# 32-wide pair attention: another order of scores and maxima on TensorE, and one buffer of probabilities in place of two

## The chip, the cores and the metric

The program runs on one core of a Trainium2 chip. The metric is the device time of one execution in microseconds, the median of the runs shown. Times are those of one hardware profile of the kernel before, unless said otherwise.

## What is computed

A decoder of two layers, each of attention, cross attention and a feed-forward part. The change touches the two self-attention cores, with 16 heads of width 32 over 4 batches of 512 positions, which per layer amount to:

```python
B, S, D, NH, HD = 4, 512, 512, 16, 32
# layer 0: one key and one value head shared by the 16 query heads; layer 1: 16 key and value heads
scores = jnp.einsum('bqhd,bkd->bhqk', Q, K) / sqrt(32)      # layer 1: 'bthd,bshd->bhts'
attn = jax.nn.softmax(scores, axis=-1)
out = jnp.einsum('bhqk,bkd->bqhd', attn, V)
```

## The kernel before

The program is a row of stages with a barrier between them; on each engine the order is written out by hand and held together by semaphores. The stage in question is `attend` (lines 376 to 666). It runs twice: tiles `l0s_...` in layer 0, `l1s_...` in layer 1. It works on 32 pairs of heads (`NP = 32`), each pair being one *step* `p`. For a pair, TensorE does

- 8 maximum matmuls (`maximum`, L460): queries by keys, 128 queries x 512 keys, two into each of the two halves of `max_bank`. VectorE reduces two of them at a time to row maxima (L604), four reductions a pair;
- `max_rows` (L470): 4 small matmuls that turn the negated maxima into two rows, which ScalarE copies into the query tile (L579), so that the score matmul subtracts them;
- 8 score matmuls (`score`, L481): keys by queries, transposed, 128 keys x 512 queries, k = 0 to 7. Even k (the pair's first head) goes to `score_bank0`, odd k to `score_bank1`. ScalarE takes the exponential of each (L590) into the probabilities `pT`;
- 4 weighings (`weigh`, L491, kt = 0 to 3), two fp32 matmuls each (every one has two rows in the profile), which multiply the values by `pT` of one block of 128 keys and add up in `o_bank`;
- `turn` (L503): 4 transposes of the result, which VectorE had copied out (`take_oT`, L622) and then divides by the sums and stores or adds (L630, L634, L640).

The work is pipelined over pairs. In step `p` TensorE works on the scores of `p`, the maxima of `p + 2`, the rows of `p + 1`, and the last weighings and the turn of `p - 1`. The steps run as 4 straight ones, a loop of 6 rounds with 4 steps (p = 4 to 27), and 4 straight ones. The last two steps have no maxima, since no pair is left. A step has two halves, which I call A (k = 0 to 3) and B (k = 4 to 7):

```python
for k in range(4):          # half A
    score(p, s, k)
    m(k)
max_rows(p + 1, ...); weigh(p - 1, ..., 2); weigh(p - 1, ..., 3)
for k in range(4, 8):       # half B
    score(p, s, k)
    m(k)
turn(p - 1); weigh(p, s, 0); weigh(p, s, 1)
```

Before each score TensorE waits until the exponential of two scores earlier has left the score bank: `pe.wait_ge(exp_done, 8 * p + k + 1)`, the counter having been started at 2. ScalarE waits for each score (`scored`), and at k = 0 also for `weighed`, the count of pairs whose last weighing is done, before it overwrites `pT[s % 2]`.

Of the kernel before, what the change touches and what calls it, by code (L numbers as in the profile page):

```python
# [374 lines left out]

def attend(st, name, q_dram, k_dram, v, per_head, out):

    nc = st.nc  # L380
    NP = B * NH // 2
    scale = HD ** -0.5
    STK = 3 * HD
    R = 4
    W = 2 * HD
    maxed, max_read, ms_ready, mrow_turned, mrow_ready, scored, exp_done, weighed, oT_ready, turned, o_read = st.sems(
        "maxed", "max_read", "ms_ready", "mrow_turned", "mrow_ready", "scored", "exp_done", "weighed", "oT_ready",
        "turned", "o_read")
    max_hi_done, rden_done, on_done, ks_made, vs_cleared, vs_made, v_staged, ms_cleared = st.sems(
        "max_hi_done", "rden_done", "on_done", "ks_made", "vs_cleared", "vs_made", "v_staged", "ms_cleared")  # L390
    loaded = st.sems(*(f"qk_loaded_{s}" for s in range(R)))
    add = out is st.x
    KN = 2 if per_head else 1
    with ExitStack() as stack:
        sb, ps = tensors(nc, stack)
        qs = [sb(f"{name}_q{s}", [P, 2, S], F32R) for s in range(R)]
        ks = [sb(f"{name}_k{s}", [P, KN, S], F32R) for s in range(R)]
        pT = [sb(f"{name}_pT{s}", [P, 2, QT, S], F32) for s in range(2)]
        mx = sb(f"{name}_mx", [P, 2, QT], F32)
        ms = [sb(f"{name}_ms{s}", [P, QT, 2, HD], F32R) for s in range(2)]  # L400
        rden = sb(f"{name}_rden", [P, QT, 2, 1], F32)
        warm = sb(f"{name}_warm", [P, 1], F32)
        on = sb(f"{name}_on", [P, QT, 2, HD], F32)
        vs = [sb(f"{name}_vs{s}", [P, QT, 2, W], F32) for s in range(2)]
        oT = sb(f"{name}_oT", [P, S], F32)
        max_bank = [ps(f"{name}_max_bank{g}", [P, 2, S]) for g in range(2)]
        score_bank = [ps(f"{name}_score_bank{g}", [P, S]) for g in range(2)]
        o_bank = ps(f"{name}_o_bank", [P, S])
        t_bank = ps(f"{name}_t_bank", [P, S])
        o4 = t_bank[:].rearrange("p (q n d) -> p q n d", q=QT, n=2)  # L410

        def rounds(eng, body):

            for s in range(R):
                body(s, s)
            with eng.Fori(1, NP // R - 1) as j:
                for s in range(R):
                    body(R * j + s, s)
            for s in range(R):
                body(NP - R + s, s)  # L420

        def early(p, n):
            return isinstance(p, int) and p < n

        def late(p, n):
            return isinstance(p, int) and p >= NP - n

        with nc.Block() as block:

            @block.sync  # L430
            def _(sp):
                def load(p, s):
                    b, h = p // (NH // 2), p % (NH // 2)
                    cols, rows = bass.ds(b * S, S), bass.ds(h * W, W)
                    q_src = q_dram[:, rows, cols].rearrange("t (n d) s -> t d n s", n=2)
                    k_src = k_dram[:, rows if per_head else slice(0, HD), cols].rearrange("t (n d) s -> t d n s", n=KN)
                    for dst, part, src in ((qs[s], 0, q_src[0]), (ks[s], 2, k_src[0])):
                        sp.dma_start(dst[part * HD:part * HD + HD].bitcast(F32), src).then_inc(loaded[s], 16)
                    for n in range(2):
                        sp.dma_start(qs[s][(n + 1) * HD:(n + 2) * HD].bitcast(F32), q_src[n]).then_inc(loaded[s], 16)  # L440
                        sp.dma_start(ks[s][n * HD:(n + 1) * HD].bitcast(F32), k_src[n]).then_inc(loaded[s], 16)

                for s in range(R):
                    load(s, s)
                with sp.Fori(1, NP // R) as j:
                    for s in range(R):
                        p = R * j + s
                        sp.wait_ge(scored, 8 * (p - R + 1))
                        load(p, s)

            @block.tensor
            def _(pe):
                def maximum(p, s, j):

                    n, q = j // QT, j % QT
                    if j == 0:
                        pe.wait_ge(loaded[s], 96 // R * (p - s) + 96)
                    if q % 2 == 0:
                        pe.wait_ge(max_read, 4 * p + j // 2 + 1)
                    ins = pe.matmul(max_bank[q // 2][:, q % 2, :], qs[s][0:STK, n, q * P:(q + 1) * P],  # L460
                                    ks[s][0:STK, n % KN, :], start=True, stop=True)
                    if q % 2:
                        ins.then_inc(maxed, 1)

                def max_rows(p, s):

                    pe.wait_ge(ms_ready, p + 1)
                    reached(pe, o_read, p - 2)
                    for q in range(QT):
                        last = pe.matmul(t_bank[0:HD + 2, q * P:(q + 1) * P],  # L470
                                         ms[s % 2][:, q, :, :].rearrange("p n w -> p (n w)")[:, 0:HD + 2],
                                         st.ident_r[:], start=True, stop=True)
                    last.then_inc(mrow_turned, 1)

                def score(p, s, k):

                    n, kt = k % 2, k // 2
                    if k == 0:
                        pe.wait_ge(mrow_ready, 2 * p + 2)
                    pe.wait_ge(exp_done, 8 * p + k + 1)  # L480
                    pe.matmul(score_bank[n][:], ks[s][0:STK + 2, n % KN, kt * P:(kt + 1) * P], qs[s][0:STK + 2, n, :],  # L481
                              start=True, stop=True).then_inc(scored, 1)

                def weigh(p, s, kt):

                    if kt == 0:
                        pe.wait_ge(v_staged, p + 1)
                        reached(pe, oT_ready, p)
                    pe.wait_ge(exp_done, 8 * p + 2 * kt + 4)
                    for n in range(2):  # L490
                        last = pe.matmul(o_bank[W * n:W * n + W, :], vs[s % 2][:, kt, n, :], pT[s % 2][:, n, kt, :],  # L491
                                         start=(kt == 0), stop=(kt == QT - 1))
                    if kt == QT - 1:
                        last.then_inc(weighed, 1)

                def turn(p):

                    pe.wait_ge(oT_ready, p + 1)
                    pe.wait_ge(mrow_ready, 2 * NP if late(p, 2) else 2 * (p + 3))
                    if late(p, 2):  # L500
                        pe.wait_ge(o_read, p)
                    for q in range(QT):
                        last = pe.transpose(t_bank[:, q * P:(q + 1) * P], oT[:, q * P:(q + 1) * P], st.ident[:])  # L503
                    last.then_inc(turned, 1)

                def step(p, s):
                    ahead, next_rows = not late(p, 2), not late(p, 1)

                    def m(j):
                        if ahead:  # L510
                            maximum(p + 2, (s + 2) % R, j)

                    for k in range(4):
                        score(p, s, k)
                        m(k)
                    if next_rows:
                        max_rows(p + 1, (s + 1) % R)
                    if not early(p, 1):
                        weigh(p - 1, (s - 1) % R, 2)
                        weigh(p - 1, (s - 1) % R, 3)  # L520
                    for k in range(4, 8):
                        score(p, s, k)
                        m(k)
                    if not early(p, 1):
                        turn(p - 1)
                    weigh(p, s, 0)
                    weigh(p, s, 1)

                for p in range(2):
                    for j in range(8):  # L530
                        maximum(p, p, j)
                pe.wait_ge(ks_made, 1)
                max_rows(0, 0)
                rounds(pe, step)
                for kt in (2, 3):
                    weigh(NP - 1, R - 1, kt)
                turn(NP - 1)

            @block.gpsimd
            def _(pool):  # L540
# [25 lines left out]
                for s in range(2):  # L566
                    stage(s, s)
# [1690 lines left out]
```

## Time and profile before

| | us |
|---|---|
| median of 3 runs | 2851.24 (2848.83 to 2853.85) |
| profiled execution, its own time | 2848.89 |
| its span in the profile | 2847.1 |
| first `l0s` score starts | 147.4 |
| last `l0s` score starts | 436.5 |
| first `l1s` score starts | 1278.5 |
| last `l1s` score starts | 1566.0 |
| TensorE busy over the whole span | 2540.0 (89%) |
| VectorE busy | 1793.7 (63%) |
| ScalarE busy | 1168.9 (41%) |

The table is read as one program with many stages, of which the two in question take some 290 us each. The share of busy time is a mean over all stages, and a TensorE matmul counts as busy while it drains, so that two matmuls in a row overlap in the profile. In the stage itself what counts is the distance from the start of one matmul to the start of the next.

### The profile page before, as it was taken

How to read it: one execution, taken by the hardware profiler on the slowest of the kernel's cores; microseconds unless marked ns; L12 is line 12 of the kernel's file. 1: busy time of each engine (PE TensorE's matmuls, PEld its weight loads, DVE VectorE, ACT ScalarE, POOL GpSimd, SP SyncE). 2: the span in 40 equal slices, each digit the busy share in tenths (PEclk: the TensorE clock that was granted, in tenths of full speed). 3: DMA queues.
4: the chain of work that ended last, by engine and by line, in shares of the span. 5: the costliest groups of instructions: out<-in, count | busy, mean ns of one | idle time of the engine just before them, and what ended most of it. 6: DMA issues, size and time to landing. Idle time of an engine off the chain costs nothing. (4 is left out here: it accounts for less than half of the span.)

```text
span 2847.1 us, 40036 instructions
## 1 busy us (share of the span) xinstructions
PE 2540.0 (89%) x11576; PEld 1827.1 (64%) x11576; DVE 1793.7 (63%) x3478; ACT 1168.9 (41%) x2283; POOL 156.2 (5%) x262
## 2 busy tenths in 40 slices
PE   4899995848999966989999869999999999999579
PEld 3644443646777755764444657777777777777457
DVE  5277776566777765236776567667666666666743
ACT  2256663313333323226665144444444444444321
POOL 0000000000000000000000310100101001010000
PEclk9989997978999988989999989999999999999789
DMA  3412211000000002333332010000000000000101
GB/s 105 129 56 62 66 50 34 1 16 1 1 0 0 0 17 100 116 111 83 85 87 56 22 38 5 15 11 7 17 5 15 11 7 11 11 7 0 39 0 60
DMA packets 71405, 103.63 MB, mean 36 GB/s; under 512 B 14399, under 2 KB 27466, under 8 KB 71214
## 3 DMA queue, kind: packets, MB, share of 16 engines
q1 hardware_dynamic: 71342, 102.82, 12.1%
q8 instruction: 35, 0.57, 0.1%
q14 instruction: 28, 0.23, 0.0%
HBM read 72.90 MB, written 29.88 MB: 36 GB/s over the span
## 5 line engine op out<-in xcount | busy, mean ns | idle before, releaser
L2151 DVE SCALAR_TENSOR_TENSOR x_res<-xa_out_bank,xa_den,x_res 128x512 f32 (+1 forms) x256 | 191.4, 748 | 155.9 <-PE xa_out_bank L1791 155.9
L2060 ACT ACTIVATE xa_pT_hi<-xa_t_bank 128x512 fp32r<-128x512 f32 x256 | 149.4, 597 | 124.9 <-PE xa_t_bank L1928 124.9
L2071 ACT ACTIVATE xa_prob<-xa_prob,xa_nmax 128x512 f32<-128x512 f32 x256 | 182.7, 715 | 30.1 <-DVE xa_nmax L2133 30.1
L1791 PE MATMUL xa_out_bank<-xa_o_w,xa_o_hi 128*128 128x512 f32 x512 | 172.3, 418 | 22.4 <-DVE x_res L2151 20.9
L2115 DVE TENSOR_TENSOR xa_pT_lo<-xa_t_bank,xa_pT_hi 128x512 fp32r<-128x512 f32 x256 | 175.7, 687 | 22.6 <-ACT xa_pT_hi L2060 18.6
L604 DVE TENSOR_REDUCE l1s_mx<-l1s_max_bank 128x2 f32<-128x1024 f32 x128 | 155.1, 1224 | 49.7 <-PE l1s_max_bank L460 49.4
L590 ACT ACTIVATE l0s_pT<-l0s_score_bank 128x512 f32<-128x512 f32 x256 | 139.3, 595 | 112.9 <-PE l0s_score_bank L481 106.6
L590 ACT ACTIVATE l1s_pT<-l1s_score_bank 128x512 f32<-128x512 f32 x256 | 139.2, 595 | 111.5 <-PE l1s_score_bank L481 105.0
L2133 DVE CUSTOM_DVE_ANT_0 xa_prob<-xa_s_bank,xa_mask_bias 128x512 f32<-128x512 f32 x256 | 171.1, 687 | 20.2 <-PE xa_s_bank L1791 9.8
L604 DVE TENSOR_REDUCE l0s_mx<-l0s_max_bank 128x2 f32<-128x1024 f32 x128 | 155.1, 1224 | 43.3 <-PE l0s_max_bank L460 43.0
L1216 DVE TENSOR_TENSOR ffn_y<-ffn_y 128x512 f32<-128x512 f32 x176 | 120.6, 690 | 70.5 <-PE ffn_y L1036 68.4
L1928 PE MATMUL xa_t_bank<-ident,xa_prob 128*128 128x128 f32 x1024 | 149.8, 274 | 0.1
L1928 PEld LDWEIGHTS xa_t_bank<-ident,xa_prob 128*128 128x128 f32 x1024 | 120.2, 140 | 39.7 <-issue 18.3
L491 PE MATMUL l0s_o_bank<-l0s_pT,l0s_vs 128*64 128x512 f32 x512 | 124.4, 607 | 0.0
L491 PE MATMUL l1s_o_bank<-l1s_pT,l1s_vs 128*64 128x512 f32 x512 | 123.8, 605 | 0.0
L1791 PEld LDWEIGHTS xa_out_bank<-xa_o_w,xa_o_hi 128*128 128x128 f32 x512 | 84.6, 190 | 57.5 <-issue 42.7
L481 PE MATMUL l0s_score_bank<-l0s_q,l0s_k 98*128 98x512 f32 x256 | 117.3, 461 | 3.6 <-ACT l0s_pT L590 1.8
L481 PE MATMUL l1s_score_bank<-l1s_q,l1s_k 98*128 98x512 f32 x256 | 116.6, 458 | 4.0 <-ACT l1s_pT L590 2.4
L2052 ACT ACTIVATE xa_q_hi<-xa_bank_a 128x512 fp32r<-128x512 f32 x64 | 38.3, 599 | 195.8 <-PE xa_bank_a L1901 195.8
L460 PE MATMUL l0s_max_bank<-l0s_k,l0s_q 96*128 96x512 f32 x256 | 106.3, 424 | 8.5 <-DMA l0s_k<-l_k 7.3
L460 PE MATMUL l1s_max_bank<-l1s_k,l1s_q 96*128 96x512 f32 x256 | 105.3, 420 | 9.4 <-DMA l1s_k<-l_k 8.4
L481 PEld LDWEIGHTS l0s_score_bank<-l0s_q,l0s_k 98*128 98x128 f32 x256 | 48.6, 191 | 96.2 <-issue 50.3
(420 smaller groups left out, 6087.2 us busy)
## 6 DMA issues: line engine op xcount, KB each, us to landing
l0s_q<-l_q SPq DMA_DIRECT2D x96, 128.0 KB, 2.3
l1s_q<-l_q SPq DMA_DIRECT2D x96, 128.0 KB, 3.0
l1s_k<-l_k SPq DMA_DIRECT2D x96, 128.0 KB, 3.2
l0s_k<-l_k SPq DMA_DIRECT2D x96, 64.0 KB, 2.4
x_res<-in_x_dram SPq DMA_DIRECT2D x1, 4096.0 KB, 13.6
l_q<-l0p_hi SPq DMA_DIRECT2D x16, 256.0 KB, 2.5
l_q<-l0p_lo SPq DMA_DIRECT2D x16, 256.0 KB, 3.0
l_q<-l1p_hi SPq DMA_DIRECT2D x16, 256.0 KB, 2.1
```

The costliest lines, as they stand in the source:

```text
L460: ins = pe.matmul(max_bank[q // 2][:, q % 2, :], qs[s][0:STK, n, q * P:(q + 1) * P], ks[s][0:STK, n % KN, :], start=True, stop=True)
L481: pe.matmul(score_bank[n][:], ks[s][0:STK + 2, n % KN, kt * P:(kt + 1) * P], qs[s][0:STK + 2, n, :], start=True, stop=True).then_inc(score ...
L491: last = pe.matmul(o_bank[W * n:W * n + W, :], vs[s % 2][:, kt, n, :], pT[s % 2][:, n, kt, :], start=(kt == 0), stop=(kt == QT - 1))
L590: act.activation(pT[s % 2][:, n, kt, :], score_bank[n][:], ACT.Exp, scale=scale)\
L604: dve.tensor_reduce(mx[:, h // 2, 2 * half:2 * half + 2], max_bank[half][:], AX.X, ALU.max)\
L1791: last = pe.matmul(bank, w, x, start=(m == 0), stop=(m == len(pairs) - 1))
L1928: last = pe.transpose(t_bank[kt % 2][:, q * P:(q + 1) * P], prob[:, q, kt * P:(kt + 1) * P], st.ident[:])
L2060: act.activation(pT_hi[:, kt % (QT - 1), :], t_bank[kt % 2][:], ACT.Copy).then_inc(pT_hi_done, 1)
L2071: act.activation(prob[:, q, :], prob[:, q, :], ACT.Exp, bias=nmax[:, q:q + 1], scale=-1.0, accum_out=den[:, r, 0, q:q + 1]).then_inc(exp_d ...
L2115: dve.tensor_tensor(lo, bank, hi.bitcast(F32), ALU.subtract).then_inc(lo_done, 1)
L2133: dve.tensor_tensor_reduce(prob[:, q, :], s_bank[q % 2][:], mask_bias[:], -scale, -LOW * 1e-5, ALU.add, ALU.min, nmax[:, q:q + 1]).then_in ...
L2151: dve.scalar_tensor_tensor(xt, out_bank[:], den[:, r, 2, q:q + 1], xt, ALU.mult, ALU.add)\
```

## The change

The stage's code becomes a class, `PairAttention`, with the same operations. What changes in what the engines are told:

```diff
-        pT = [sb(f"{name}_pT{s}", [P, 2, QT, S], F32) for s in range(2)]
+        self.pT = sb(f"{name}_pT", [P, 2, QT, S], F32)
...
-                    for k in range(4):
-                        score(p, s, k)
-                        m(k)
+            def half(k, j):
+                self.score(pe, p, s, k)
+                self.score(pe, p, s, k + 1)
+                m(j)
+                m(j + 1)
+                m(j + 2)
+                self.score(pe, p, s, k + 2)
+                m(j + 3)
+                self.score(pe, p, s, k + 3)
+
+            half(0, 0)
...
-                    for k in range(4, 8):
-                        score(p, s, k)
-                        m(k)
+            half(4, 4)
...
-                    if kt == QT - 1:
-                        last.then_inc(weighed, 1)
+        if kt % 2:
+            last.then_inc(self.weighed, 1)
...
-                        if k == 0:
-                            reached(act, weighed, p - 1)
+                if k % 4 == 0:
+                    reached(act, self.weighed, 2 * p - 1 + k // 4)
...
-                act.sem_inc(exp_done, 2)
...
-                dve.sem_inc(max_read, 2)
...
-                    pe.wait_ge(exp_done, 8 * p + k + 1)
+        reached(pe, self.exp_done, 8 * p + k - 1)
...
-                    reached(pool, weighed, p - 1)
+            reached(pool, self.weighed, 2 * p - 2)
...
-                    dve.wait_ge(weighed, p + 1)
+        dve.wait_ge(self.weighed, 2 * p + 2)
```

The two counters that started at 2 now start at 0, and their thresholds are lower by 2. `weighed` counts two for each pair: one after kt = 1, one after kt = 3. With one buffer, the exponentials k = 0 to 3 of pair `p` overwrite the blocks kt = 0 and 1 of pair `p - 1`, and so wait for its weighing kt = 1; the exponentials k = 4 to 7 wait for its weighing kt = 3.

TensorE's order in half A of the loop's second step (p = 5, 9, ...; `score_bank0` takes even k), before:

```order
L481 MATMUL l0s_score_bank0<-l0s_q1,l0s_k1 128x512 [waits exp_done_30]
L459 ISA [waits qk_loaded_3_46]
L460 MATMUL l0s_max_bank0<-l0s_k3,l0s_q3 128x512 [waits max_read_25]
L480 REGISTER_ALU
L481 MATMUL l0s_score_bank1<-l0s_q1,l0s_k1 128x512 [waits exp_done_30]
L460 MATMUL l0s_max_bank0<-l0s_k3,l0s_q3 128x512
L480 REGISTER_ALU
L481 MATMUL l0s_score_bank0<-l0s_q1,l0s_k1 128x512 [waits exp_done_30]
L459 REGISTER_ALU
L460 MATMUL l0s_max_bank1<-l0s_k3,l0s_q3 128x512 [waits max_read_25]
L480 REGISTER_ALU
L481 MATMUL l0s_score_bank1<-l0s_q1,l0s_k1 128x512 [waits exp_done_30]
```

and now:

```order
L479 MATMUL l0s_score_bank0<-l0s_q1,l0s_k1 128x512 [waits exp_done_30]
L479 MATMUL l0s_score_bank1<-l0s_q1,l0s_k1 128x512 [waits exp_done_30]
L75 ISA [waits qk_loaded_3_46]
L458 MATMUL l0s_max_bank0<-l0s_k3,l0s_q3 128x512 [waits max_read_25]
L458 MATMUL l0s_max_bank0<-l0s_k3,l0s_q3 128x512
L458 MATMUL l0s_max_bank1<-l0s_k3,l0s_q3 128x512 [waits max_read_25]
L75 REGISTER_ALU
L479 MATMUL l0s_score_bank0<-l0s_q1,l0s_k1 128x512 [waits exp_done_30]
L458 MATMUL l0s_max_bank1<-l0s_k3,l0s_q3 128x512
L75 REGISTER_ALU
L479 MATMUL l0s_score_bank1<-l0s_q1,l0s_k1 128x512 [waits exp_done_30]
```

Three maxima now stand between the second and the third score, where one stood; the half's fourth maximum stands between the third and the fourth score, and nothing follows the fourth score.

ScalarE's order at the start of the same step of the loop, before:

```order
L587 ISA
L590 ACTIVATE l0s_pT<-l0s_score_bank 128x512 [waits weighed_31,scored_29]
L587 REGISTER_ALU
L590 ACTIVATE l0s_pT<-l0s_score_bank 128x512 [waits scored_29]
```

and now:

```order
L590 ISA
L75 ISA [waits scored_29]
L593 ACTIVATE l0s_pT<-l0s_score_bank 128x512 [waits weighed_31]
L590 REGISTER_ALU
L593 ACTIVATE l0s_pT<-l0s_score_bank 128x512 [waits scored_29]
```

In the second, third and fourth step of the loop the wait for the first score of half A moved from the exponential to an instruction of the sequencer ahead of it. In the loop's first step the wait stood on such an instruction before, too (a REGISTER_ALU there, an ISA now). The first exponential of half B has both waits on itself.

## Rows read from the trace of the kernel before

**Rows 1.** Waits, 170 to 430 us: engine, line, waited for, total us, times, longest.

```profile
PEld l0s_score_bank L481 <- ACT l0s_pT L590: 36.3, 114, 0.9
```

**Rows 2.** Timeline of TensorE, half A of p = 13 and B's first: start us, us, what.

```profile
267.40 0.50 PE L481 MATMUL l0s_score_bank<-l0s_q,l0s_k 98*128 98x512 f32 x1
267.73 0.40 PE L460 MATMUL l0s_max_bank<-l0s_k,l0s_q 96*128 96x512 f32 x1
267.97 0.40 PE L481 MATMUL l0s_score_bank<-l0s_q,l0s_k 98*128 98x512 f32 x1
268.21 0.40 PE L460 MATMUL l0s_max_bank<-l0s_k,l0s_q 96*128 96x512 f32 x1
268.58 0.51 PE L481 MATMUL l0s_score_bank<-l0s_q,l0s_k 98*128 98x512 f32 x1
268.93 0.40 PE L460 MATMUL l0s_max_bank<-l0s_k,l0s_q 96*128 96x512 f32 x1
269.16 0.40 PE L481 MATMUL l0s_score_bank<-l0s_q,l0s_k 98*128 98x512 f32 x1
269.40 0.40 PE L460 MATMUL l0s_max_bank<-l0s_k,l0s_q 96*128 96x512 f32 x1
269.64 0.40 PE L470 MATMUL l0s_t_bank<-ident_r,l0s_ms 128*34 128x128 f32 x4
269.97 1.94 PE L491 MATMUL l0s_o_bank<-l0s_pT,l0s_vs 128*64 128x512 f32 x8
271.84 0.50 PE L481 MATMUL l0s_score_bank<-l0s_q,l0s_k 98*128 98x512 f32 x1
```

**Rows 3.** Timeline of the weight loads of the third and fourth score there.

```profile
268.58 0.19 PEld L481 LDWEIGHTS l0s_score_bank<-l0s_q,l0s_k 98*128 98x128 f32 x1 [0.42 <-ACT l0s_pT L590]
...
269.06 0.19 PEld L481 LDWEIGHTS l0s_score_bank<-l0s_q,l0s_k 98*128 98x128 f32 x1 [0.19 <-ACT l0s_pT L590]
```

**Rows 4.** Timeline of ScalarE: p = 12 (four together), then the first two of p = 13.

```profile
258.85 2.28 ACT L590 ACTIVATE l0s_pT<-l0s_score_bank 128x512 f32<-128x512 f32 x4 [2.45 <-PE l0s_score_bank L481]
...
267.93 0.60 ACT L590 ACTIVATE l0s_pT<-l0s_score_bank 128x512 f32<-128x512 f32 x1 [2.37 <-PE l0s_score_bank L481]
...
268.42 0.59 ACT L590 ACTIVATE l0s_pT<-l0s_score_bank 128x512 f32<-128x512 f32 x1
```

**Rows 5.** Timeline of TensorE, p = 30 (no maxima), and the start of p = 31.

```profile
422.21 0.73 PE L481 MATMUL l0s_score_bank<-l0s_q,l0s_k 98*128 98x512 f32 x2
...
423.39 0.99 PE L481 MATMUL l0s_score_bank<-l0s_q,l0s_k 98*128 98x512 f32 x2 [0.45 <-ACT l0s_pT L590]
...
424.22 0.41 PE L470 MATMUL l0s_t_bank<-ident_r,l0s_ms 128*34 128x128 f32 x4
...
430.83 0.73 PE L481 MATMUL l0s_score_bank<-l0s_q,l0s_k 98*128 98x512 f32 x2
```

**Rows 6.** Timeline: first scores of p = 1, 4, 12 and 16.

```profile
158.05 0.50 PE L481 MATMUL l0s_score_bank<-l0s_q,l0s_k 98*128 98x512 f32 x1
...
185.34 0.50 PE L481 MATMUL l0s_score_bank<-l0s_q,l0s_k 98*128 98x512 f32 x1
...
258.23 0.50 PE L481 MATMUL l0s_score_bank<-l0s_q,l0s_k 98*128 98x512 f32 x1
...
294.68 0.50 PE L481 MATMUL l0s_score_bank<-l0s_q,l0s_k 98*128 98x512 f32 x1
```

**Rows 7.** Windows of the first step (p = 0) and of steady steps: PEclk is the granted clock.

```profile
147.00:156.90 9.90, 9.43 (x24) 5.82 (x26) 5.26 (x7) 6.16 (x11) 0.00 (x0) 0.50 0.02 7
170.00:430.00 260.00, 258.73 (x1138) 123.25 (x1136) 192.47 (x283) 157.73 (x286) 15.34 (x58) 1.00 0.19 59
```

**Rows 8.** Timeline of VectorE in half B of p = 13.

```profile
271.96 0.69 DVE L622 COPY l0s_oT<-l0s_o_bank 128x512 f32<-128x512 f32 x1 [0.90 <-PE l0s_o_bank L491]
273.07 2.44 DVE L604 TENSOR_REDUCE l0s_mx<-l0s_max_bank 128x2 f32<-128x1024 f32 x2 [0.42 <-PE l0s_max_bank L460]
...
276.75 0.42 DVE L634 TENSOR_TENSOR l0s_on<-l0s_t_bank,l0s_rden 128x256 f32<-128x256 f32 x1
```

More of the change, by code:

```diff
@@ L376, in attend @@
 def attend(st, name, q_dram, k_dram, v, per_head, out):
     nc = st.nc
[L381 to L390, printed above, removed]
@@ L428, in attend @@
+    with ExitStack() as stack:
+        att = PairAttention(st, stack, name, q_dram, k_dram, v, per_head, out)
         with nc.Block() as block:
@@ L431, in _ @@
             def _(sp):
[L432 to L449, printed above, removed]
+                att.first_loads(sp)
+                att.loads(sp)
             @block.tensor
             def _(pe):
[L453 to L463, printed above, removed]
@@ L484, in weigh @@
[L484 to L492, printed above, removed]
-                    if kt == QT - 1:
-                        last.then_inc(weighed, 1)
@@ L496, in turn @@
[L496 to L511, printed above, removed]
-                    for k in range(4):
-                        score(p, s, k)
-                        m(k)
[L516 to L520, printed above, removed]
-                    for k in range(4, 8):
-                        score(p, s, k)
-                        m(k)
[L524 to L527, printed above, removed]
@@ L529, in _ @@
                 for p in range(2):
                     for j in range(8):
[L531 to L537, printed above, removed]
+                        att.maximum(pe, p, p, j)
+                pe.wait_ge(att.ks_made, 1)
+                att.max_rows(pe, 0, 0)
+                att.tensor(pe)
@@ L566, in _ @@
-                for s in range(2):
-                    stage(s, s)
-                with pool.Fori(1, NP // 2) as j:
-                    for s in range(2):
-                        stage(2 * j + s, s)
+                att.make_constants(pool)
+                att.stage_values(pool)
             @block.scalar
             def _(act):
-                act.sem_inc(exp_done, 2)
-                def rows(p, s):
-                    act.wait_ge(mrow_turned, p + 1)
-                    for n in range(2):
-                        act.activation(qs[s][STK:STK + 2, n, :], t_bank[HD * n:HD * n + 2, :], ACT.Copy)\
-                            .then_inc(mrow_ready, 1)
@@ L582, in step @@
-                def step(p, s):
-                    for k in range(8):
-                        n, kt = k % 2, k // 2
-                        if k == 4 and not late(p, 1):
-                            rows(p + 1, (s + 1) % R)
-                        act.wait_ge(scored, 8 * p + k + 1)
-                        if k == 0:
-                            reached(act, weighed, p - 1)
-                        act.activation(pT[s % 2][:, n, kt, :], score_bank[n][:], ACT.Exp, scale=scale)\
-                            .then_inc(exp_done, 1)
@@ L593, in _ @@
[L593 to L595 removed]
+                act.activation(att.warm[:], st.ident[:, 0:1], ACT.Exp)
+                att.rows(act, 0, 0)
+                att.scalar(act)
             @block.vector
             def _(dve):
[L599 to L605 removed]
```

350 lines of the change are left out of this document (225 added, 125 removed).

## Prediction, made before the changed kernel ran

> **What bounds the stage.** I read the windows first, then the waits, then the timelines of one step engine by engine. [...]
>
> The timeline of one half says what these waits cost [rows 2]. Take the first score as time 0. Matmuls that follow each other without a wait start 0.23 to 0.24 apart (0.33, 0.57, 0.81), and the small ones of `max_rows` would come in the same rhythm. But the third score starts at 1.18 instead of 1.04. It is released by the first exponential, which starts at 0.53 and takes 0.60 [rows 4], so ends at 1.13; 0.05 later the load starts. Nothing hides that load, so the matmul really begins 0.10 after it: the next one comes at 1.53, 0.35 behind the third score where 0.24 is the rule. That half loses 0.14 + 0.10 = 0.24 us there, the price of one matmul slot. The fourth score's load also starts late, at 1.66 [rows 3], released by the second exponential (1.02 + 0.59 = 1.61), but its matmul at 1.76 is in rhythm with the third maximum (1.53 + 0.23), so this wait costs nothing. The block `max_rows` begins at 2.24, and half B at 4.44.
>
> The reader should see one more thing: step 30 does the same without any maximum [rows 5]. Its scores stand at 0, 0.34 (two in one row), 1.18 and 1.67, and `max_rows` at 2.01; its full step takes 430.83 - 422.21 = 8.62 us. That is the floor that the exponentials set. A step with maxima takes (185.34 - 158.05) / 3 = 9.10, and a loop round of four takes 294.68 - 258.23 = 36.45 [rows 6]. Three of its steps take 9.09 each ((294.68 - 267.40) / 3, with [rows 2]), the first 9.17.
>
> **Part 1: the order on TensorE.** No matmul is added or dropped. The new half is: score 0 at 0, score 1 at 0.34, three maxima at 0.57, 0.81 and 1.04, and the third score's slot at 1.28. Its release at 1.18 plus the bare load of 0.10 is also 1.28: the three maxima just fill the hole that the first exponential leaves. The fourth maximum comes at 1.52; the fourth score is ready at 1.67 + 0.10 = 1.77 against a slot of 1.75. Then `max_rows` starts at 2.01 instead of 2.24: one slot, 0.23 to 0.24 us, won in each half. The new step is thus the floor of 8.62 us with all maxima in its holes, 0.47 below 9.09. ScalarE gains nothing and loses nothing: its second exponential follows the first by 0.49 both in step 13 (score 1 at 0.57) and in step 30 (at 0.34), so an earlier score 1 does not move it.
>
> [...]
>
> **Part 2: the waits on ScalarE.** In the loop's first step the first exponential started 258.85 - 258.23 = 0.62 after its score, against 0.53 in step 13 [rows 4, 6]: 0.08 to 0.09 for a wait that a sequencer instruction holds ahead of the exponential. That step is 0.08 longer. In the new order of instructions all four steps of the loop have such a wait at the start of half A. So each step of the loop takes 8.62 + 0.08 = 8.70, and the gain is 0.39 in three of four steps and 0.47 in the first. Half B keeps its wait on the exponential; from no row but the straight steps do I know that a double wait there is free (step 30, at k = 0: 0.54). Its bounds are 0 and 0.08; I take 0, the nearer row.
>
> **Part 3: one buffer of probabilities.** The exponentials of half A now wait for the previous pair's weighing kt = 1, the last group on TensorE before score 0; those of half B for kt = 3, the last group before score 4. That group ends at 269.97 + 1.94 = 271.91 [rows 2], 0.07 after the next score starts, and VectorE reacts at 271.96 [rows 8]. ScalarE needs the score itself anyway, at 0.53. So the release is there 0.4 us early. Cost 0; if that cover went, every half would pay the lateness. The second increment of `weighed` rides on a matmul. VectorE, GpSimd and the loads on SP have the same releases as before, and no DMA is moved past anything.
>
> **What is late next.** VectorE: from 273.07 to the end of L634 at 277.17 it works nearly without a break, 4.1 us [rows 8]. Its next reduction waits for the second maximum of the next half A, which stands at 0.81 as before. From one such start to the next it is the length of half B: 9.09 - (271.84 - 267.40) = 4.65 us today [rows 2, 6], 0.24 less afterwards, 4.41. So VectorE fits, with 0.3 to spare. Even a late reduction would hurt nobody: TensorE needs that bank only a half later.
>
> **The sum.** [...] Steps 30 and 31 have no maxima: 0. Straight steps 1, 2, 3, 28, 29: 5 x 0.47 = 2.35. Loop: 6 x (36.45 - 4 x 8.70) = 9.9. Together 12.25 us a layer; layer 1 has the same order of TensorE (its loads of keys are wider, its output isn't added to x), so twice: **24.5 us**. Against the profiled execution, 2848.89, that gives 2824.4; its time lies 2.35 below the median of the runs, 2851.24, against which I predict **2826.7**.
>
> **The rivals.**
> 1. *The hole is filled, but part is given back.* The double wait in half B costs 0.08 in the loop (24 x 2 x 0.08 = 3.8 us), and the fourth score's load, now at the edge (1.77 against 1.75), shows 0.10 in each of the 116 halves of the 29 steps and two layers (11.6 us). For: both are within 0.02 us of deciding. Against: step 30 has `max_rows` at 2.01 with just these releases. Time 2826.7 + 3.8 to 11.6, so 2830.5 to 2838.3. Chance 0.10.
> 2. *Only the wait of 0.14 us is won, not the bare load of 0.10*: 116 x 0.14 - 2.9 (the 36 halves of part 2 that lose 0.08) = 13.3 us come off: 2837.9. For: the third score's load is still released by an exponential, and still bare. Against: its matmul begins at 1.28 with that load counted [rows 2, 3], in the slot that three maxima leave it. Chance 0.03. [...]
> 3. *The single buffer makes ScalarE wait: slower.* Place: the first exponential of each half. The release must come later than 0.43 us after the weighing's end before it costs anything, and later than 0.43 + 0.21 = 0.64 (24.5 / 116 = 0.21) before the change turns slower. If it came one pair of weighings late (1.94 / 2 = 0.97), each of 116 halves would pay 0.54, in all 63 us, less 24.5: 2890. For: this wait is new, and the text puts the last weighing right ahead of the score. Against: VectorE reacts to the same signal within 0.05. Chance 0.04.
> 4. *No change that can be seen*, because something else, VectorE for instance, turns out to hold the step at 9.09: 2851. Against: its 0.9 and 0.42 us of idle time in half B [rows 8]. Chance 0.03.
>
> **How the numbers follow.** The forecast has 0.80. [...] So 2820 to 2834; that takes in the mild end of rival 1 and leaves out the rest, less than 2 in 10. Faster by over 0.2% (5.7 us, about what a measurement of this kernel can tell from none): the forecast, rivals 1 and 2, 0.93. Within it: 0.03. Slower: 0.04.
>
> **What would show it.** In the profile after, a steady half has scores at 0, 0.34, 1.18 (1.26 in half A of the loop) and 1.76 (1.84), maxima at 0.57, 0.81, 1.04 and 1.52, `max_rows` or `turn` at 2.01 (2.09); four loop steps take 34.8 us; the waits of score loads for exponentials stay in number but shrink; the first exponential starts 0.53 to 0.62 behind its score. The prediction is wrong if the first exponential starts later than 0.62, if the three maxima don't stand 0.24 apart, or if steps stay above 8.8 us.

## The result, and the profile after

| | before | after |
|---|---|---|
| median of 4 runs each, us | 2850.57 (2848.83 to 2853.85) | 2829.82 (2828.72 to 2832.05) |
| ratio, 95% interval | | 0.9927, 0.991 to 0.9944 |
| span of the profiled execution, us | 2847.1 | 2828.7 |
| its mean granted clock | 0.947 | 0.946 |
| steps 1 to 29 of layer 0, us | 264.16 | 251.94 |
| the same of layer 1 | 264.13 | 252.07 |

The change is faster by 20.75 us between the medians, and by 18.4 between the spans. I had forecast 2826.7, in a range from 2820 to 2834.

The sequence on TensorE is shorter while its matmuls are as many. This is the page of the kernel after, busy time by engine:

```profile
PE 2521.1 (89%) x11576; PEld 1829.5 (65%) x11576; DVE 1785.6 (63%) x3478; ACT 1169.2 (41%) x2283; POOL 156.2 (6%) x262
```

The timeline of TensorE in step 13, half A and half B, answers to [rows 2] (start us, us, engine, line, what, count):

```profile
261.24 0.73 PE L479 MATMUL l0s_score_bank<-l0s_q,l0s_k 98*128 98x512 f32 x2
261.81 0.87 PE L458 MATMUL l0s_max_bank<-l0s_k,l0s_q 96*128 96x512 f32 x3
262.52 0.50 PE L479 MATMUL l0s_score_bank<-l0s_q,l0s_k 98*128 98x512 f32 x1
262.85 0.40 PE L458 MATMUL l0s_max_bank<-l0s_k,l0s_q 96*128 96x512 f32 x1
263.09 0.41 PE L479 MATMUL l0s_score_bank<-l0s_q,l0s_k 98*128 98x512 f32 x1
263.34 0.40 PE L468 MATMUL l0s_t_bank<-ident_r,l0s_ms 128*34 128x128 f32 x4
263.67 1.94 PE L489 MATMUL l0s_o_bank<-l0s_pT,l0s_vs 128*64 128x512 f32 x8
265.54 0.50 PE L479 MATMUL l0s_score_bank<-l0s_q,l0s_k 98*128 98x512 f32 x1
...
266.79 0.43 PE L479 MATMUL l0s_score_bank<-l0s_q,l0s_k 98*128 98x512 f32 x1
...
267.55 0.60 PE L501 MATMUL l0s_t_bank<-ident,l0s_oT 128*128 128x128 f32 x4
...
269.94 0.50 PE L479 MATMUL l0s_score_bank<-l0s_q,l0s_k 98*128 98x512 f32 x1
```

From the first score the third stands at 262.52 - 261.24 = 1.28, the fourth at 1.85 and `max_rows` at 2.10. In half B the third score stands at 1.25 and `turn` at 2.01. Half A takes 4.30 (before 4.44), half B 4.40 (before 4.65), the step 8.70. The weight loads of the third and fourth score of that half answer to [rows 3]:

```profile
262.51 0.19 PEld L479 LDWEIGHTS l0s_score_bank<-l0s_q,l0s_k 98*128 98x128 f32 x1 [0.27 <-ACT l0s_pT L593]
...
263.00 0.19 PEld L479 LDWEIGHTS l0s_score_bank<-l0s_q,l0s_k 98*128 98x128 f32 x1 [0.19 <-ACT l0s_pT L593]
```

The third score still waits, 0.27 instead of 0.42 [rows 3], and its load is still bare: the next maximum starts 0.33 behind it, not 0.24. The waits of the steady stretch, 158 to 420 us (total us, times, longest), answer to [rows 1]:

```profile
PEld l0s_score_bank L479 <- ACT l0s_pT L593: 27.6, 122, 0.9
```

As many waits as before, some two per half, but 0.23 each where it was 36.3 / 114 = 0.32. The single buffer shows on ScalarE. Its timeline in the same half answers to [rows 4], that of VectorE in half B to [rows 8]:

```profile
261.86 2.27 ACT L593 ACTIVATE l0s_pT<-l0s_score_bank 128x512 f32<-128x512 f32 x4 [2.22 <-PE l0s_score_bank L479]
```

```profile
265.65 0.69 DVE L622 COPY l0s_oT<-l0s_o_bank 128x512 f32<-128x512 f32 x1 [0.82 <-PE l0s_o_bank L489]
266.76 2.36 DVE L604 TENSOR_REDUCE l0s_mx<-l0s_max_bank 128x2 f32<-128x1024 f32 x2 [0.41 <-PE l0s_max_bank L458]
```

The first exponential starts 0.62 behind its score, where step 13 had 0.53. VectorE's reduction starts 1.22 behind the half's first score as before and still waits 0.41 for its maxima, so VectorE did not become late.

### The profile page after: what moved, and what is told of

It is laid out like the page before. It is cut to its first block and busy times, and to the rows that moved or that the text cites. A ratio compares the mean times of both kernels' runs of the same rounds, so it can differ in the third digit from the quotient of the medians.

```text
span 2828.7 us, 40026 instructions
## 1 busy us (share of the span) xinstructions
PE 2521.1 (89%) x11576; PEld 1829.5 (65%) x11576; DVE 1785.6 (63%) x3478; ACT 1169.2 (41%) x2283; POOL 156.2 (6%) x262
## 5 line engine op out<-in xcount | busy, mean ns | idle before, releaser
L1966 PEld LDWEIGHTS xa_t_bank<-ident,xa_prob 128*128 128x128 f32 x1024 | 120.2, 140 | 40.0 <-issue 18.4
L1978 PE MATMUL xa_o_bank<-xa_pT_hi,xa_v_hi 128*128 128x512 f32 x256 | 108.8, 425 | 0.1
L1829 PE MATMUL xa_s_bank<-xa_k_hi,xa_q_hi 128*128 128x512 f32 x256 | 106.3, 415 | 2.2 <-DVE xa_q_lo L2153 2.0
L479 PE MATMUL l1s_score_bank<-l1s_q,l1s_k 98*128 98x512 f32 x256 | 105.1, 451 | 3.1 <-ACT l1s_pT L593 1.8
L479 PE MATMUL l0s_score_bank<-l0s_q,l0s_k 98*128 98x512 f32 x256 | 104.9, 451 | 3.1 <-ACT l0s_pT L593 1.8
L1939 PE MATMUL xa_bank_a<-xa_xT_hi,xa_q_w 128*128 (+1 forms) x320 | 104.6, 392 | 0.0
```

Of the source, the lines that this page charges most:

```text
L479: pe.matmul(self.score_bank[n][:], self.ks[s][0:self.STK + 2, n % self.KN, kt * P:(kt + 1) * P], self.qs[s][0:self.STK + 2, n, :], start=T ...
L1829: last = pe.matmul(bank, w, x, start=(m == 0), stop=(m == len(pairs) - 1))
L1966: last = pe.transpose(t_bank[kt % 2][:, q * P:(q + 1) * P], prob[:, q, kt * P:(kt + 1) * P], st.ident[:])
```

## The experiments

Twelve more runs were made: nine further kernels, one of them twice, and the kernel after twice more. "Steps 1 to 29" is always the distance from the first score of step 1 to the first score of step 30, so the 29 steps with maxima, which ran at the full granted clock (1.00 from 158.05 to 422.21 us before, 1.00 from 157 to 409 us after): some 264.15 us a layer before, 252.0 after. Where the clock rose late, step 1 began at a granted clock of 0.50 and is longer (8.75 us in layer 1 of the kernel after, 9.04 in layer 0 of the one with swapped waits).

### The order alone, and the buffer alone

The kernel before, with two buffers of probabilities, gets only the new order:

```diff
-                    for k in range(4):
-                        score(p, s, k)
-                        m(k)
+                    score(p, s, 0)
+                    score(p, s, 1)
+                    m(0)
+                    m(1)
+                    m(2)
+                    score(p, s, 2)
+                    m(3)
+                    score(p, s, 3)
```

(and half B likewise).

> The kernel before with the new order on TensorE alone (two buffers of probabilities, waits as before). My theory: the whole gain is the order's. Steps with maxima fall to 8.62 us, and only the first of four loop steps stands at 8.70, since ScalarE's sequencer wait is there alone; a loop round takes 34.6 us, the two stages together are 24.5 + 2.9 = 27.4 us shorter than before. Rival (the one buffer has part in the gain): less is won here than in the changed kernel, whose loop round takes 34.8 us.

The kernel after gets the old order back:

```diff
-                self.score(pe, p, s, k)
-                self.score(pe, p, s, k + 1)
-                m(j)
-                m(j + 1)
-                m(j + 2)
-                self.score(pe, p, s, k + 2)
-                m(j + 3)
-                self.score(pe, p, s, k + 3)
+                for i in range(4):
+                    self.score(pe, p, s, k + i)
+                    m(j + i)
```

> The changed kernel with score and maximum in turn again (one buffer, its waits). My theory: no gain; the wait at the start of half A costs 0.08 us in three more steps of the loop, so a loop round takes 36.7 us instead of 36.45, and the two stages 2.9 us more than before. Rival (the single buffer itself makes ScalarE wait): first exponentials later than 0.62 us behind their score, and steps above 9.17.

| | median, us | ratio to before, 95% | steps 1 to 29, layers 0 and 1 |
|---|---|---|---|
| order alone | 2825.73 (5 runs) | 0.9916, 0.9903 to 0.993 | 250.43, 250.67 |
| buffer alone | 2855.68 (11 runs) | 1.0017, 1.0008 to 1.0026 | 265.28, 265.32 |

The order carries the whole gain. A round of the loop in the timeline of the kernel with the order alone, first scores of p = 12 and 16:

```profile
252.61 0.50 PE L481 MATMUL l0s_score_bank<-l0s_q,l0s_k 98*128 98x512 f32 x1
...
287.16 0.50 PE L481 MATMUL l0s_score_bank<-l0s_q,l0s_k 98*128 98x512 f32 x1
```

That is 34.55: three steps of 8.62 and the loop's first of 8.69, as it had its wait on the sequencer before too. In the kernel after the same round takes the 34.80 of these rows of its timeline:

```profile
252.54 0.50 PE L479 MATMUL l0s_score_bank<-l0s_q,l0s_k 98*128 98x512 f32 x1
...
287.34 0.50 PE L479 MATMUL l0s_score_bank<-l0s_q,l0s_k 98*128 98x512 f32 x1
```

The buffer alone costs time. In its timeline of step 13, the first exponential comes 265.93 - 265.31 = 0.62 behind the score:

```profile
265.31 0.50 PE L479 MATMUL l0s_score_bank<-l0s_q,l0s_k 98*128 98x512 f32 x1
```

```profile
265.93 0.60 ACT L588 ACTIVATE l0s_pT<-l0s_score_bank 128x512 f32<-128x512 f32 x1 [2.45 <-PE l0s_score_bank L479]
```

Its loop steps take 9.16 to 9.18, its straight ones 9.08. The price is 1.15 us a layer under the old order and 1.5 under the new one (252.0 - 250.5). The working of part 2 gives 18 steps times 0.08, so 1.44: six rounds, three steps in each that did not pay it before. So what the single buffer costs in the steps is the place of a wait. The median went up by more, some 5 us; in the profiled execution 2.3 of the 6.0 by which the span is longer lie in these steps and 4.8 outside the two stages (2223.26 against 2218.48 before), while step 0 of layer 0 was 1.6 shorter; more on this below.

### The two waits of an exponential, swapped

```diff
-                act.wait_ge(self.scored, 8 * p + k + 1)
                 if k % 4 == 0:
                     reached(act, self.weighed, 2 * p - 1 + k // 4)
+                act.wait_ge(self.scored, 8 * p + k + 1)
```

> The changed kernel with ScalarE's two waits in the other order: the weighing first, on the sequencer, then the score, on the exponential. My theory: the first exponential of half A starts 0.53 us after its score in every step, all steps with maxima take 8.62, and the two stages are 24 x 0.08 x 2 = 3.8 us shorter than in the changed kernel. Rival (the 0.08 us come from somewhere else, such as the loop's registers): 8.70 stays.

Measured: 2827.51 (5 runs), ratio 0.9923 (0.9909 to 0.9937); steps 1 to 29 take 251.04 and 250.74. Timelines of step 13 and, behind the dots, of the straight steps 28 and 29, TensorE and then ScalarE:

```profile
262.88 0.50 PE L479 MATMUL l0s_score_bank<-l0s_q,l0s_k 98*128 98x512 f32 x1
...
392.28 0.50 PE L479 MATMUL l0s_score_bank<-l0s_q,l0s_k 98*128 98x512 f32 x1
...
401.02 0.50 PE L479 MATMUL l0s_score_bank<-l0s_q,l0s_k 98*128 98x512 f32 x1
```

```profile
263.42 0.60 ACT L593 ACTIVATE l0s_pT<-l0s_score_bank 128x512 f32<-128x512 f32 x1 [2.13 <-PE l0s_score_bank L479]
...
392.88 0.60 ACT L593 ACTIVATE l0s_pT<-l0s_score_bank 128x512 f32<-128x512 f32 x1 [2.19 <-PE l0s_score_bank L479]
```

In the loop the exponential is back at 0.54 and the step at 8.63. What I had not expected are the straight steps: the exponential moved from 0.54 to 0.60 there, and the step from 8.63 to 401.02 - 392.28 = 8.74, since the first exponential of half B is late too (0.59).

### How wide the hole is

Three kernels measure the hole that the first exponential leaves. In the first two, the second maximum of each half's four is sent twice, with the same operands into the same bank: once in the old order, once in the new. The page of both counts 11704 matmuls instead of 11576, so 128 more, one for each half's four maxima. The expectations speak of two for each half; that count of mine was wrong.

```diff
-                    ins = pe.matmul(max_bank[q // 2][:, q % 2, :], qs[s][0:STK, n, q * P:(q + 1) * P],
-                                    ks[s][0:STK, n % KN, :], start=True, stop=True)
+                    for _ in range(2 if q == 1 else 1):
+                        ins = pe.matmul(max_bank[q // 2][:, q % 2, :], qs[s][0:STK, n, q * P:(q + 1) * P],
+                                        ks[s][0:STK, n % KN, :], start=True, stop=True)
```

> The kernel before, in which each second maximum of a pair of maxima is sent twice into the same bank (116 more matmuls between the second and the third score in the two stages' steady steps, 128 in all, and as many behind each half's last score). My theory: the one between the second and third score falls into the hole and costs nothing; the one behind the half's last score costs a slot of 0.235 us. So a half goes from 4.44 to 4.68 us and a step from 9.09 to 9.56. Rival (the hole is no room for a matmul, the wait and the load stay): both cost a slot, the step takes 10.03.

> The changed kernel with the same maxima sent twice. My theory: the hole is full already, so both extra matmuls of a half cost a slot of 0.235 us each (the last of them partly hidden behind the wait of the fourth score): half A goes from 4.29 to about 4.75 us, a step from 8.70 to about 9.6. Rival (room is left): the step stays below 9.2.

The third kernel puts only two maxima ahead of the third score:

```diff
                 m(j + 1)
-                m(j + 2)
                 self.score(pe, p, s, k + 2)
+                m(j + 2)
                 m(j + 3)
```

> The changed kernel with the order score, score, maximum, maximum, score, maximum, maximum, score. My theory: the hole before the third score is filled but for one slot; its load stands bare again, and the fourth score comes a slot later than its exponential needs. The third score stands at 1.18 (half B), max_rows or turn at 2.24, a loop step at 9.1 to 9.2 us: all of the gain is gone. Rival (it is enough that two scores come first): 8.7 to 8.8.

Timelines of TensorE in step 13: the old order with an extra maximum,

```profile
267.12 0.50 PE L482 MATMUL l0s_score_bank<-l0s_q,l0s_k 98*128 98x512 f32 x1
...
267.92 0.63 PE L461 MATMUL l0s_max_bank<-l0s_k,l0s_q 96*128 96x512 f32 x2
...
269.36 0.40 PE L471 MATMUL l0s_t_bank<-ident_r,l0s_ms 128*34 128x128 f32 x4
```

the new order with it,

```profile
268.57 0.73 PE L480 MATMUL l0s_score_bank<-l0s_q,l0s_k 98*128 98x512 f32 x2
269.14 1.09 PE L459 MATMUL l0s_max_bank<-l0s_k,l0s_q 96*128 96x512 f32 x4
270.07 0.40 PE L480 MATMUL l0s_score_bank<-l0s_q,l0s_k 98*128 98x512 f32 x1
...
270.79 0.40 PE L469 MATMUL l0s_t_bank<-ident_r,l0s_ms 128*34 128x128 f32 x4
```

and the new order with two maxima first:

```profile
266.68 0.74 PE L479 MATMUL l0s_score_bank<-l0s_q,l0s_k 98*128 98x512 f32 x2
267.26 0.63 PE L458 MATMUL l0s_max_bank<-l0s_k,l0s_q 96*128 96x512 f32 x2
267.95 0.50 PE L479 MATMUL l0s_score_bank<-l0s_q,l0s_k 98*128 98x512 f32 x1
268.29 0.63 PE L458 MATMUL l0s_max_bank<-l0s_k,l0s_q 96*128 96x512 f32 x2
268.76 0.40 PE L479 MATMUL l0s_score_bank<-l0s_q,l0s_k 98*128 98x512 f32 x1
269.00 0.41 PE L468 MATMUL l0s_t_bank<-ident_r,l0s_ms 128*34 128x128 f32 x4
```

| order of a half | `max_rows` at | step in the loop | time, us (1 run) | before beside it |
|---|---|---|---|---|
| old, one maximum more | 2.24 | 9.08 (9.17 in the first) | 2850.94 | 2850.77 |
| new, one maximum more | 2.22 | 9.02 | 2850.41 | 2850.77 |
| new, two maxima first | 2.32 | 9.13 | 2856.45 | 2850.02 |

The same matmul is free in the old order (2.24 is also where `max_rows` stood before) and costs 2850.41 - 2829.82 = 20.6 us in the new one. The hole was there, one slot wide, and the new order has used it. By its steps (261.58 against 251.94 in layer 0) the price is 9.6 a layer, so 9.6 / 58 = 0.17 for each half, not a whole slot of 0.24. It is a mean of two cases. In the straight steps (9.03 against 8.63) and in half B of the loop it is some 0.20: with four maxima ahead the third score stands at 1.50, its load is no longer late, and the next matmul comes 0.21 later than in the kernel after. In half A of the loop it is 0.12 (2.22 against 2.10), because the extra matmul also covers the 0.08 of the sequencer's wait: all steps of this kernel take 9.02 to 9.03, in the loop and outside it.

With two maxima first the hole is open again: the third score waits to 1.27, its load is bare (the next maximum at 1.61), and both remaining maxima stand behind it. The step loses its gain, and with the sequencer's wait on top steps 1 to 29 take 264.49 and 264.58, 0.8 us in sum more than before. The run was 6.4 us slower than before; the rest of that lies outside these steps. So two maxima ahead of the third score are too few, and a fourth matmul in that place costs time when it is an extra one. Whether all four maxima ahead of the third score would do as well as three was not tried.

### The exponential late on purpose

The first exponential of each half waits for the second score too, so that it starts later with nothing else changed:

```diff
-                act.wait_ge(self.scored, 8 * p + k + 1)
+                act.wait_ge(self.scored, 8 * p + k + (2 if k % 4 == 0 else 1))
```

> The changed kernel, in which the first exponential of each half waits for the second score too, as if the buffer of probabilities came free late. My theory (rival 3's price): the second score ends at 0.34 + 0.40, so the first exponential starts at 0.78 in half B (0.25 later) and at 0.86 in half A of the loop (0.24 later), and each half gets longer by just that: a loop step goes from 8.70 to about 9.2 us, the whole is some 28 us longer than the changed kernel and no faster than the kernel before. Rival (there is slack between the exponentials and TensorE): less than half of that.

Timelines of step 13, TensorE and ScalarE:

```profile
267.24 0.73 PE L479 MATMUL l0s_score_bank<-l0s_q,l0s_k 98*128 98x512 f32 x2
...
271.76 0.50 PE L479 MATMUL l0s_score_bank<-l0s_q,l0s_k 98*128 98x512 f32 x1
```

```profile
268.09 0.60 ACT L593 ACTIVATE l0s_pT<-l0s_score_bank 128x512 f32<-128x512 f32 x1 [2.45 <-PE l0s_score_bank L479]
```

The exponential starts at 0.85 instead of 0.62, 0.23 later, and half A takes 4.52 instead of 4.30, 0.22 longer. Steps 1 to 29 take 265.48 and 265.56, in sum 27.0 us more than after: 0.23 for each of 116 halves. The whole takes 2857.88 (1 run), 28 us more. ScalarE has no slack in this order at the three delays that were run: 0.06 (the straight steps with swapped waits, 0.11 a step), 0.08 (the loop) and 0.23 each came out in the halves in full. This also bears out the point of rival 3: at about 0.21 late the gain is gone, and this kernel, 0.23 late, has steps that are 2.8 us in sum longer than before.

### Step 0, both mended, and the same kernel again

The first kernel of this group keeps the old order in step 0 alone:

```diff
             def half(k, j):
+                if self.early(p, 1):
+                    for i in range(4):
+                        self.score(pe, p, s, k + i)
+                        m(j + i)
+                    return
```

> The changed kernel, but with score and maximum in turn in the first step (p = 0) of each stage alone. [...] So step 0 comes back to 9.0 to 10.7 us, and the whole is some 3 us shorter than the changed kernel. Rival (the clock's rise falls at a random moment, and the lengths of step 0 with it): step 0 stays spread up to 11.5 and nothing is won.

The 9.0 to 10.7 us are what step 0 took with the old order, 10.67 and 9.13 before and 9.04 and 9.13 with the buffer alone; 11.5 is the longest that it took in the kernel after.

The second has that, and in the loop, not in the straight steps, the wait for `weighed` written before the one for `scored`. It ran twice.

> As the run before, and in the loop ScalarE waits for the weighing on its sequencer and for the score on the exponential (in the straight steps the reverse, as in the changed kernel). My theory: all steps with maxima take 8.62 or 8.63 us, 3.8 us less in all than in the run before, some 7 us less than the changed kernel: about 2823 to 2825. Rival: the parts do not add up, since later stages take back what is won.

> The version with the first step in turn and the waits in the better order, once more, beside the changed kernel on the same chip. In the first profile its two stages took 4.5 us less than the changed kernel's, but the rest of the program 2227.6 us, where the other profiles have 2218 to 2223. [...] Rival: the rest is again near 2227, the shorter stages are paid for later, and the median equals the changed kernel's.

The kernel after ran twice more, unchanged.

> The changed kernel as it is, once more, for its time on the same chip and a second profile. [...]

> The changed kernel a third time, for the comparison with the run before. My theory: steady steps of 8.70 us; rest of the program somewhere between 2218 and 2224 us; step 0 of each stage 10.4 to 11.5 us; median 2829 to 2832.

"Rest" is the span of the profiled execution without the two stages that the change touches, each taken from its first matmul to the first of the next stage; step 0 is given for layers 0 and 1.

| | median, us (5 runs; before and after 4) | span | steps 1 to 29 | rest | step 0 |
|---|---|---|---|---|---|
| before | 2850.57 | 2847.1 | 264.16, 264.13 | 2218.48 | 10.67, 9.13 |
| after | 2829.82 | 2828.7 | 251.94, 252.07 | 2222.80 | 10.40, 11.50 |
| after, second time | 2831.61 | 2824.0 | as after | 2218.40 | 10.77, 10.40 |
| after, third time | 2827.26 | 2827.9 | as after | 2224.77 | 9.09, 10.30 |
| old order in step 0 | 2828.75 | 2826.8 | as after | 2221.88 | 10.80, 9.14 |
| both mended | 2829.68 | 2828.9 | 250.13, 250.12 | 2227.64 | 11.01, 9.14 |
| both mended, again | 2827.31 | 2827.9 | 249.98, 249.99 | 2226.32 | 10.97, 10.75 |

Two things follow. The mended kernel has every steady step at 8.62 or 8.63, in straight code and in the loop, and its steps are 3.8 to 4.0 us shorter in sum than those of after. That is as expected. But its medians, 2829.68 and 2827.31, lie among those of the kernel after, 2827.26 to 2831.61: no gain that can be measured, though I had expected the second to be some 4 us below the kernel after. In both its profiled executions the rest took 2226 to 2228, the longest of all. Two profiles of a kernel do not settle whether that is chance or a consequence, and why it would be one stays open.

Whether the old order in step 0 brought the 3 us that I expected of it can't be told from the medians: 2828.75 lies among the three of the kernel after. Step 0 of layer 1 was at its old length, that of layer 0 was not.

## Why the prediction was right, and where it was off

**What bounds the kernel, part 1, and the floor: right.** The new half was predicted at 0, 0.34, 1.18 (1.26), 1.76 (1.84) and 2.01 (2.09); in half A of step 13, which has the bracketed ones, the trace has the third load at 1.27, and then 1.85 and 2.10. In half B only the third score differs: its load starts at 1.18, but the matmul stands at 1.25. The list of signs put the matmul at 1.18; part 1, with its slot at 1.28, had it nearly right. The order alone gives steps of 8.62, the floor of step 30 [rows 5]. That the hole of one slot was there is shown by the extra maximum that costs nothing in the old order; that it is filled, by the same one costing 0.17 a half in the new.

The slot's size is settled as well. Matmul starts stand 0.23 to 0.24 apart in every timeline above, and with the order alone, which leaves the waits as they were, a half became one such slot shorter: (264.15 - 250.55) / 58 halves = 0.234. That TensorE's own sequence sets the pace [rows 7] is borne out by the same figure: one slot less in its order is one slot less in the half.

**Part 2, the wait on the sequencer: right in place and size.** 0.08 in 18 more steps a layer was in the sum; the order alone against after shows 1.5 us a layer, 1.44 worked out. That the second wait in half B costs nothing held too, though for another reason than I gave: there the sequencer's instruction waits for `weighed`, which has come by 0.12, and the exponential starts 0.53 behind the score. The price of a wait on the sequencer, when the later event is the one waited for there, was 0.08 in the loop (0.62 against 0.54) and 0.06 in the straight steps (0.60 against 0.54).

**Part 3, the single buffer: right.** The release comes early enough: where the sequencer's instruction waits for `weighed` it is through 0.12 behind the score, some 0.4 ahead of the exponential. The kernel with the buffer alone is 2.3 us longer in its steps, all from the wait's place. Rival 3 did not come, and the late exponential shows that lateness is paid in full: 0.23 late cost 0.23 in each half.

**Rivals 1, 2 and 4** fell. Rival 1 had the fourth score's load late in each half: the fourth score is followed by `max_rows` 0.25 behind it (263.34 - 263.09), so nothing is bare there. (Its two prices, 3.8 and 11.6, could have come together; the range given for it leaves that out.) Rival 2 had only the wait won: half B shrank by 0.25, not by 0.14. Rival 4 had VectorE hold the step; it waits for TensorE as before.

**The sum: right in the steps, off outside them.** 24.5 us were predicted, and steps 1 to 29 are shorter by 12.22 + 12.06 = 24.3. But the medians differ by 20.75 and the spans by 18.4. What failed is that the sum counts no change for all else, step 0 first. No run shows that step 0 stays as it was: in layers 0 and 1 it took 10.67 and 9.13 before, 10.40 and 11.50 after. These windows hold the long stretch from the start of the stage `xa` to that of `mix`, then the stage `fa` behind the first attention, then step 0 of layer 1 (from:to, length, busy us of PE, PEld, DVE, ACT and POOL, granted clock, DMA share, GB/s). Before:

```profile
1639.54:2671.82 1032.28, 976.26 (x4704) 770.71 (x4704) 701.95 (x1443) 480.77 (x1019) 76.65 (x82) 0.98 0.04 13
455.46:597.42 141.96, 102.89 (x452) 80.38 (x452) 83.18 (x153) 44.86 (x87) 0.00 (x0) 0.86 0.04 8
1278.49:1287.62 9.13, 8.54 (x29) 5.09 (x29) 5.25 (x6) 5.73 (x10) 0.00 (x0) 0.74 0.04 12
```

After:

```profile
1618.16:2653.16 1035.00, 978.50 (x4704) 771.79 (x4704) 702.07 (x1443) 480.85 (x1019) 76.53 (x82) 0.98 0.04 13
442.47:586.89 144.42, 101.18 (x452) 79.10 (x453) 84.31 (x153) 44.75 (x87) 0.00 (x0) 0.87 0.04 8
1267.06:1278.56 11.50, 11.50 (x28) 6.08 (x29) 5.24 (x6) 5.73 (x10) 0.00 (x0) 0.50 0.12 35
```

The same kernel after, when it ran a second time:

```profile
1616.29:2648.52 1032.23, 976.73 (x4705) 771.12 (x4705) 701.61 (x1443) 480.71 (x1019) 76.66 (x82) 0.98 0.04 13
442.89:585.46 142.57, 102.05 (x452) 79.54 (x453) 84.55 (x153) 44.79 (x87) 0.00 (x0) 0.86 0.04 8
1267.18:1277.58 10.40, 10.40 (x29) 6.01 (x29) 5.23 (x6) 5.73 (x10) 0.00 (x0) 0.56 0.07 18
```

Step 0 of layer 1 ran at 0.74 of full clock before and at 0.50 after: the clock rose 4.83 us behind the step's first score before, 11.81 after. That is 2.37 of the missing us. The long stretch, in which nothing changed, took 1032.28 before and 1035.00 after (2.72 more); it spent 39.0 us at a granted clock of 0.50 before and 48.6 after. In the second execution it took 1032.23, with 39.0 at the lower level. Over all fourteen traces the four with 39.0 to 39.3 us at the lower level have 1032.2 to 1032.6 for this stretch, the ten with 44.0 to 52.7 us have 1033.9 to 1035.7. So its length goes with the time at the lower level, and one kernel can have either. `fa` took 2.46 more after, at no lower clock; it too differs between executions of one kernel (144.42, 142.57 and 141.48), and why was not looked into. The spans of the three profiles of after go from 2824.0 to 2828.7 with nearly equal steps.

But it is not chance alone. Take steps 1 to 29 of both layers off each median. The kernel before, in its four groups of runs, has 2321.7 to 2322.5 us left; the kernel after, in three, 2325.8, 2327.7 and 2323.4; all other kernels, the one with the old order and one buffer too (2325.1), 2323.1 to 2329.4. Not one comes down to the kernel before. So every kernel that was changed in this stage took back 0.6 to 7 us elsewhere, against the kernel before beside it, where the sum has 0 and the range left room for a few us either way. That room either way was my estimate, and no run shows it: by these medians the rest was only ever longer. The three medians of the kernel after, 2827.26, 2829.82 and 2831.61, lie 0.6 to 4.9 above the forecast, all within that range, and all on the same side.

**What stays open.** Whether the new order itself delays the clock's rise in step 0. Leave out the kernels of extra or late work and the one with two maxima first: five executions have the new order in step 0, five the old one. In layer 0 they do not differ, with means of 10.54 and 10.50 us. In layer 1 they do: 10.30 to 11.50 (mean 10.89) with the new order, where the clock rose 9.0 to 12.1 us behind the first score; 9.13 or 9.14 in four with the old order, where it rose after 4.8 to 5.8, and 10.75 in the fifth, where it rose after 9.7 (mean 9.46). That points to the order as the cause of some 1.4 us in layer 1, from five executions against five; how it would delay the rise, and why in one layer alone, no run shows. The rest of what every changed kernel takes back outside its steps is open as well.

**Is there a better version?** The order with two buffers had the lowest median of all, 2825.73 against 2827.26 to 2831.61 of the kernel after. The 3 us that its steps are shorter are shown in the trace; beside the second time of the kernel after, in the same group of runs, its median was 5.9 us lower, beside the third time, in another group, 1.5. In the medians they are at the edge of what the runs scatter.

## What to carry to other kernels

When another engine releases a weight load late, look at more than the wait. Here the load itself was bare as well, and the two together cost one matmul slot of 0.234 us in each half. Look for the gap between the matmul behind the load and the one that the load feeds, and put independent matmuls ahead of it until the gap is filled: here two were too few, three fitted, and an extra one beyond them cost 0.12 to 0.20 us. When a busy share near 100% hides stalls, as 258.73 of 260 us [rows 7] did with 36.3 us of late weight loads behind it [rows 1], a step of the same kernel that lacks part of the work, here the last ones without maxima, shows the floor before anything is run. When an instruction has two waits, find in the trace which of them the sequencer takes; the event that comes last should be the one on the instruction itself; otherwise the exponentials here started 0.06 to 0.08 us later. And read a change of 10 or 20 us in one stage from that stage's steps, but don't take what is missing in the whole for noise before several kernels have been compared: here the rest of the program was 0.6 to 7 us longer in every changed kernel.

## What the runs showed of the hardware

- **The place of the later wait.** An exponential with two waits started 0.53 to 0.54 behind its score when the sequencer's instruction ahead of it waited for `weighed`, which had come long before, and the exponential for the score. When the sequencer's instruction waited for the score, the exponential started at 0.62 in the loop and at 0.60 in the straight steps. Which wait went where was opposite in the loop and in straight code for the same order in the text.
- **Equal kernels, unequal stages.** A stage of 1032.2 us with 39.0 us at a granted clock of 0.50 took 1035.7 with 52.7 there in another execution of the same kernel. The mean clock of the whole execution, 0.947 and 0.944, hardly shows it. Four of fourteen executions had 39.0 to 39.3 us at 0.50 there and at most 1032.6 us, ten had 44.0 to 52.7 and at least 1033.9.
- **A bare weight load.** The matmul behind a third score whose load was released late stood 0.33 to 0.35 us after it, where 0.23 to 0.24 is the spacing without a wait: 0.10 us for a load of 128 columns, beside the wait.
